# Silu experts with 352 rows per expert and an output projection in three fp16 matmuls

## The reference, cut to what matters

```python
# L3_ffn: 8 experts, top 2 per token, C = 128, hidden size H = 341
flat = layer_norm(t).reshape(-1, C)
probs = softmax(flat @ router_w.T)
topk_probs, topk_idx = top_k(probs, 2)
gates = scatter(topk_probs / (sum(topk_probs) + 1e-9))      # (tokens, 8), zero where not chosen
h = silu(einsum('nc,ehc->neh', flat, w1)) * einsum('nc,ehc->neh', flat, w3)
y = einsum('neh,ech->nec', h, w2)
t = t + einsum('ne,nec->nc', gates, y)
```

## Time and profile before

| | us |
|---|---|
| median of 3 runs | 4210.65 (4209.47 to 4216.52) |
| the profiled execution | 4210.06, span of the core 4208.3 |
| PE busy | 3396.0 (81%) |
| DVE, ACT, POOL busy | 2493.0 (59%), 1934.1 (46%), 862.6 (20%) |
| stage silu_experts | from about 3378.5 to the end |
| its POOL multiply, x352 | 451.6, mean 1.285 |
| its DVE multiply, x352 | 243.5, mean 0.692 |
| its ACT silu, x352 | 210.2, mean 0.597 |

### The profile page before, as it was taken

The page is one execution under the profiler, slowest core; times in us unless marked ns, Lnnn a source line. Parts: engine busy times, 40 slices in busy tenths (PEclk is TensorE's granted clock), DMA queues, the critical chain, the costliest instruction groups (busy, mean ns, idle before and its releaser), DMA issues. The chain is left out here.

```text
span 4208.3 us, 66480 instructions
## 1 busy us (share of the span) xinstructions
PE 3396.0 (81%) x24463; PEld 1527.2 (36%) x24463; DVE 2493.0 (59%) x4082; ACT 1934.1 (46%) x2321; POOL 862.6 (20%) x866
## 2 busy tenths in 40 slices
PE   6988777557687777777777777779978659999999
PEld 4655455324211111111111111253366524444444
DVE  3227667465588888888888888344367523333333
ACT  1215666512156666666666666533333213223332
POOL 0001333300000000000000000004400225555555
PEclk9997878878789999999999999979998779999999
DMA  4444454300400000000000000014400122322221
GB/s 138 132 120 95 108 113 109 84 1 6 174 11 14 20 18 22 20 14 20 17 22 15 20 15 15 19 34 153 138 1 0 42 78 80 97 89 84 85 82 47
DMA packets 137544, 247.17 MB, mean 59 GB/s; under 512 B 34808, under 2 KB 47264, under 8 KB 136800
## 3 DMA queue, kind: packets, MB, share of 16 engines
q1 hardware_dynamic: 137312, 243.98, 20.5%
HBM read 171.55 MB, written 56.62 MB: 54 GB/s over the span
## 5 line engine op out<-in xcount | busy, mean ns | idle before, releaser
L1073 DVE TENSOR_REDUCE mxv<-mx_ps 128x1 f32<-128x512 f32 x2048 | 1279.6, 682 | 240.7 <-PE mx_ps L932 240.6
L1048 ACT ACTIVATE PT<-st_ps 128x1024 f32<-128x1024 f32 x1024 | 992.5, 1021 | 450.2 <-PE st_ps L945 444.4
L932 PE MATMUL mx_ps<-KS,QS 24*128 24x512 f16 x2048 | 538.0, 391 | 318.0 <-DVE mxv L1073 300.4
L1921 DVE TENSOR_TENSOR u<-h_ps,s 128x512 f32<-128x512 f32 x352 | 243.5, 692 | 541.2 <-ACT s L1899 492.8
L959 PE MATMUL o_ps<-PT,VA 128*32 128x512 f32 x4096 | 547.2, 606 | 1.1 <-ACT PT L1048 0.9
L1951 POOL TENSOR_TENSOR hg<-u,gb 128x512 f32<-128x512 f32 x352 | 451.6, 1285 | 392.6 <-DVE u L1921 300.2
L1899 ACT ACTIVATE s<-h_ps 128x512 f32<-128x512 f32 x352 | 210.2, 597 | 586.9 <-PE h_ps L1875 586.9
L667 DVE TENSOR_REDUCE mxv<-mx_ps 128x4 f32<-128x512 f32 x512 | 319.9, 683 | 150.3 <-PE mx_ps L542 139.2
L1883 PE MATMUL y_ps<-hg,m_w 128*128 128x512 f32 x704 | 360.7, 596 | 56.4 <-POOL hg L1951 56.4
L932 PEld LDWEIGHTS mx_ps<-KS,QS 24*128 24x128 f16 x2048 | 136.9, 91 | 568.3 <-DVE mxv L1073 530.7
L945 PE MATMUL st_ps<-QS,KS 26*128 26x512 f16 x2048 | 326.9, 382 | 1.0 <-ACT PT L1048 0.2
(11 more groups left out here) (228 smaller groups left out, 4172.9 us busy)
## 6 DMA issues: line engine op xcount, KB each, us to landing
gb<-g SPq DMA_DIRECT2D x64, 512.0 KB, 3.7
gb<-g SPq DMA_DIRECT2D x16, 2048.0 KB
QK<-qk SPq DMA_DIRECT2D x128, 192.0 KB
qk<-hl SPq DMA_DIRECT2D x80, 256.0 KB, 3.3
RB<-d SPq DMA_DIRECT2D x48, 256.0 KB, 3.4
qk<-hl SPq DMA_DIRECT2D x64, 128.0 KB, 3.3
v<-vs SPq DMA_DIRECT2D x32, 256.0 KB
VS<-v SPq DMA_DIRECT2D x32, 256.0 KB, 3.1
```

Source lines behind the costliest of these rows:

```text
L932: nc.tensor.matmul(mx_ps[:, use % 3, :], rows(QS, g // 2, j, STACK)[:, t * C:(t + 1) * C], rows(KS, g // 2, j, STACK)[:, half * HALF:(half ...
L1048: nc.scalar.activation(PT[:, n % 2, 2 * a:2 * a + 2], st_ps[:, a], ACT.Exp, scale=1.0 / SHIFT ** 2).then_inc(st_free[a], 1)
L1073: nc.vector.tensor_reduce(mxv[:, g % 2, j, t, half:half + 1], mx_ps[:, slot], AX.X, ALU.max).then_inc(mx_free, 1)
```

## The change

Each expert is padded from 341 to 352 rows; 8 x 352 = 2816 rows are again 22 chunks. Six chunks are mixed instead of 7 (the cut at 1408 falls between chunks), with cuts at 96, 64, 32, 96, 64 and 32 rows, so 12 partial loads per half image instead of 14.

w2 is split too, times 256 into two fp16 parts. y(n) becomes three fp16 matmuls: w2 high and w2 low with the rounded hidden values `hh`, and w2 high with their rest `hl`. ACT makes hh(n) from hg(n) after silu(n+2), DVE makes hl(n) = hg(n) - hh(n) after u(n+2), and y follows h with a lag of four steps. hg has two slots instead of four, so hg(n) now waits for hl(n-2), where it waited for y(n-4). The order runs on across images: the last four y of an image stand between the first h of the next, and the second half is added at step 5 of the next image instead of after the last step. The first half is added at step 27 of its image, where it was at step 25.

w1 and w3 are loaded during the norm of O, rounded by ACT at its end (`early`), and subtracted and scaled by POOL during the last norm (`late`). w2 is loaded during the last norm; in `route` ACT first multiplies and rounds it, then stages XN, and POOL makes its rest. The gelu mixture's route, too, now rounds its weights before it stages XN.

```diff
-HID = 341
-CHUNKS = -(-E * HID // C)
+HID, HID_ROWS = 341, 352
+CHUNKS = E * HID_ROWS // C
 LO = 2.0 ** 11
+W2_UNIT = 2.0 ** 8
...
+            if late is not None:
+                @block.gpsimd
+                def _(pool):
+                    late.subtract(pool)
+
...
+                if early is not None:
+                    early.round(act)
...
+                if late is not None:
+                    late.set_lift()
...
+        self.nc, self.dram, self.split, self.plain = chip.nc, dram, split, plain
+        self.unit, self.lift_by = unit, lift
...
+    def round(self, act):
+
+        act.wait_ge(self.loaded, 16 * (len(self.split) + len(self.plain)))
+        for n, (_, hi, _) in enumerate(self.split):
+            if self.unit != 1.0:
+                self.nc.scalar.mul(self.full[:, n], self.full[:, n], self.unit).then_inc(self.scaled, 1)
+                act.wait_ge(self.scaled, n + 1)
+            self.nc.scalar.copy(hi, self.full[:, n]).then_inc(self.rounded, 1)
+
+    def set_lift(self):
+
+        self.nc.vector.memset(self.lift[:], self.lift_by).then_inc(self.set, 1)
+
+    def subtract(self, pool):
+
+        pool.wait_ge(self.set, 1)
+        for n, (_, hi, lo) in enumerate(self.split):
+            pool.wait_ge(self.rounded, n + 1)
+            self.nc.gpsimd.tensor_tensor(self.full[:, n], self.full[:, n], hi, ALU.subtract).then_inc(self.rest, 1)
+            pool.wait_ge(self.rest, n + 1)
+            copy_scaled(self.nc, lo, self.full[:, n], self.lift).then_inc(self.done, 1)
+        pool.wait_ge(self.done, len(self.split))
...
             def _(pool):
-                pool.wait_ge(lifted, 1)
...
-                sp.wait_ge(weights.loaded, weights.count)
...
             @block.scalar
             def _(act):
+                weights.round(act)
                 with act.Fori(0, B // 2) as i:
                     for s in range(2):
                         act.wait_ge(logits, i * 2 + s + 1)
                         nc.scalar.copy(xs[:, s], XN[:, i * 2 + s, :]).then_inc(staged, 1)
-                act.wait_ge(weights.loaded, weights.count)
-                for n, (_, hi, _) in enumerate(weights.split):
-                    nc.scalar.copy(hi, weights.full[:, n]).then_inc(w_hi, 1)
                 act.wait_ge(chain, 2)
...
-    first, last = c * C // HID, min((c + 1) * C, E * HID) - 1
-    return first, last // HID, (first + 1) * HID - c * C
...
-    H_SLOTS, HG_SLOTS, LAG = 2, 4, 2
+    H_SLOTS, P_SLOTS, CAST, LOW, LAG = 2, 4, 2, 2, 4
...
+        hg = chip.buf(ctx, "hg", [C, H_SLOTS, HALF])
+        hh, hl = (chip.buf(ctx, n, [C, P_SLOTS, HALF], F16) for n in ("hh", "hl"))
...
+                def output(i, n):
+                    s, c = n // CHUNKS, n % CHUNKS
+                    if c == 0:
+                        pe.wait_ge(added, i * 2 + s + 1)
+                    pe.wait_ge(rest, i * PER + n + H_SLOTS + 1)
+                    nc.tensor.matmul(y_ps[:, s], w2h[:, c, :], hh[:, n % P_SLOTS], start=(c == 0), stop=False)
+                    nc.tensor.matmul(y_ps[:, s], w2l[:, c, :], hh[:, n % P_SLOTS], start=False, stop=False)
+                    nc.tensor.matmul(y_ps[:, s], w2h[:, c, :], hl[:, n % P_SLOTS], start=False,
+                                     stop=(c == CHUNKS - 1)).then_inc(y_steps, 1)
+
+                def image(i, first):
+                    for n in range(PER):
+                        hidden_rows(i, n)
                         if n >= LAG:
-                            m = n - LAG
-                            s, c = m // CHUNKS, m % CHUNKS
-                            if c == 0:
-                                pe.wait_ge(added, i * 2 + s + 1)
-                            pe.wait_ge(gated, i * PER + m + H_SLOTS + 1)
-                            nc.tensor.matmul(y_ps[:, s], w2[:, c, :], hg[:, m % HG_SLOTS], start=(c == 0),
-                                             stop=(c == CHUNKS - 1)).then_inc(y_steps, 1)
-
-                with pe.Fori(0, B) as i:
-                    image(i)
+                            output(i, n - LAG)
+                        elif not first:
+                            output(i - 1, PER + n - LAG)
+
+                image(0, True)
+                with pe.Fori(1, B) as i:
+                    image(i, False)
+                for n in range(PER - LAG, PER):
+                    output(B - 1, n)
...
-                def image(i, last):
+                def round_hidden(i, n):
+                    act.wait_ge(gated, i * PER + n + H_SLOTS + 1)
+                    act.wait_ge(y_steps, i * PER + n + 1)
+                    nc.scalar.copy(hh[:, n % P_SLOTS], hg[:, n % H_SLOTS]).then_inc(cast, 1)
+
+                def image(i, first, last):
                     for n in range(PER):
                         act.wait_ge(h_ready, i * PER + n + 1)
                         nc.scalar.activation(s1[:, n % H_SLOTS], h_ps[:, n % H_SLOTS, 0], ACT.Silu).then_inc(silu_done, 1)
+                        if n >= CAST:
+                            round_hidden(i, n - CAST)
+                        elif not first:
+                            round_hidden(i - 1, PER + n - CAST)
                         if n == CHUNKS // 2:
...
+                image(0, True, False)
+                with act.Fori(1, B - 1) as i:
+                    image(i, False, False)
+                image(B - 1, False, True)
+                for n in range(PER - CAST, PER):
+                    round_hidden(B - 1, n)
...
-                def image(i, last):
+                def rest_of_hidden(i, n):
+                    v.wait_ge(cast, i * PER + n + 1)
+                    v.wait_ge(y_steps, i * PER + n + 1)
+                    nc.vector.tensor_tensor(hl[:, n % P_SLOTS], hg[:, n % H_SLOTS], hh[:, n % P_SLOTS],
+                                            ALU.subtract).then_inc(rest, 1)
+
+                def add(i, s):
+                    v.wait_ge(y_steps, i * PER + (s * CHUNKS + CHUNKS + P_SLOTS))
+                    at = X[:, i, s * HALF:(s + 1) * HALF]
+                    nc.vector.scalar_tensor_tensor(at, y_ps[:, s], 1 / W2_UNIT, at, ALU.mult, ALU.add).then_inc(added, 1)
+
+                def image(i, first, last):
                     for n in range(PER):
                         v.wait_ge(silu_done, i * PER + n + 1)
                         v.wait_ge(gated, i * PER + n + 1)
                         nc.vector.tensor_tensor(u[:, n % H_SLOTS], h_ps[:, n % H_SLOTS, 1], s1[:, n % H_SLOTS],
                                                 ALU.mult).then_inc(hidden, 1)
+                        if n >= LOW:
+                            rest_of_hidden(i, n - LOW)
+                        elif not first:
+                            rest_of_hidden(i - 1, PER + n - LOW)
                         if n == CHUNKS // 2:
                             low(i, 1)
                         if n == CHUNKS // 2 + CHUNKS and not last:
                             low(i + 1, 0)
+                        if n == LAG + 1 and not first:
+                            add(i - 1, 1)
...
-                            v.wait_ge(y_steps, i * PER + (CHUNKS + HG_SLOTS))
-                            at = X[:, i, 0:HALF]
-                            nc.vector.tensor_tensor(at, y_ps[:, 0], at, ALU.add).then_inc(added, 1)
-                    v.wait_ge(y_steps, i * PER + (PER + HG_SLOTS))
-                    at = X[:, i, HALF:N]
-                    nc.vector.tensor_tensor(at, y_ps[:, 1], at, ALU.add).then_inc(added, 1)
...
+                grant(nc, scratch, [(hidden, H_SLOTS), (gated, H_SLOTS), (rest, H_SLOTS), (y_steps, P_SLOTS), (added, 2)])
                 low(0, 0)
-                with v.Fori(0, B - 1) as i:
-                    image(i, False)
...
+                with v.Fori(1, B - 1) as i:
+                    image(i, False, False)
+                image(B - 1, False, True)
+                for n in range(PER - LOW, PER):
+                    rest_of_hidden(B - 1, n)
+                add(B - 1, 1)
...
-                        pool.wait_ge(y_steps, i * PER + n + 1)
-                        nc.gpsimd.tensor_tensor(hg[:, n % HG_SLOTS], u[:, n % H_SLOTS], gb[:, s, tile],
+                        pool.wait_ge(rest, i * PER + n + 1)
+                        nc.gpsimd.tensor_tensor(hg[:, n % H_SLOTS], u[:, n % H_SLOTS], gb[:, s, tile],
                                                 ALU.mult).then_inc(gated, 1)
...
+            wh, wl = (chip.buf(c2, n, [C, 2, CHUNKS, C], F16) for n in ("m3_wh", "m3_wl"))
+            w2h, w2l = (chip.buf(c2, n, [C, CHUNKS, C], F16) for n in ("m3_w2h", "m3_w2l"))
...
+                inner = Weights(chip, c3, dram, [(f"m3_w{2 * n + 1}", flat(wh[:, n]), flat(wl[:, n])) for n in range(2)], lift=LO)
+                with ExitStack() as c4:
+                    O = chip.buf(c4, "O", [C, B, N])
+                    local_attention(chip, XN, dram, identf, O)
+                    layer_norm(chip, O, mean_w, eps5, identf, X=X, gamma=gamma, beta=beta, fetch=inner, early=inner)
```

(64 more changed lines are left out.)

50 lines of the change are left out of this document (13 added, 37 removed).

## The result

| | before | changed |
|---|---|---|
| median | 4212.34 (4209.47 to 4216.52, 4 runs) | 4087.78 (4085.09 to 4091.84, 4 runs) |
| the profiled execution | 4210.06, span 4208.3 | 4087.38, span 4085.6 |
| stage: first gate issue | 3378.72 | 3369.37 |
| first hg | 3424.10 | 3386.26 |
| first hg to the end of the span | 784.2 | 699.3 |

A forecast was written before the change was run, and what follows sets the result against it. PE's matmul stream was taken as the bound: 3396.4 + 676.7 + 6.3 = 4079.4, with 3.97 after it 4083.4, less 6.6 a span of 4076.8, median 4079 us. Own range 4068 to 4090; with rivals 4066 to 4116.

The forecast's parts named there:

- The stream: Last stage, PE: a step falls from ten slots to nine, 1.937 us; 3144 slots, 676.7 us, remain.
- the sum: Forecast total: 4083.4 less 6.6 gives a span of 4076.8 us, 131.5 less than 4208.3.
- the loop heads: PE's loop jump at image ends: up to 0.32 us may show, six times, 1.9 us.
- The turn of hl and hg: Last stage, DVE and POOL alternate: 1.90 us a step, 0.04 under PE; nothing counted, +8 kept in the range.
- Rival 1: Loop heads and after xl: PE waits 2 to 4 us an image, +16 to +30, about 4100; chance 0.12.
- Rival 2: Last stage: hl and hg become the bound, a turn of 2.12 us, +64, 4143; chance 0.12.
- The gate load: Start of last stage: 3.67 MB over all sixteen engines lands 15.5 us after issue, at 3394.2.
- Ahead of the stage: Route, gelu route and norm of O before the last stage: together -6.6 us.
- Route's chain: Route, DVE: four operations beside POOL's splitting return to 0.69 us each, 12.7 us off the path.
- The norms: Norm of O covers ACT's 5.0 us but for 0.3; POOL's splitting beside the last norm costs nothing, 22 at most.
- rival 4: Ahead of the stage: the edit gives nothing back, POOL slows the last norm, +8 to +22, about 4093; chance 0.03.
- Rival 3: Last stage: partial loads stay on few engines, 45.4 us each, half images 54.3; 4274, 64 slower; chance 0.03.

The follow-up runs named there:

- e1: Changed kernel with four slots for hg instead of two; ratio to the kernel before 0.9678, first hg to end 689.6 us.
- e2: Changed kernel with hl computed from a zero tile in PSUM minus hh, its low part left out of the result; ratio 0.9654, first hg to end 689.9 us.
- e7: Changed kernel with w1 and w3 loaded during the last norm and split beside route again; ratio to the kernel before 0.9747.
- e4: Changed kernel with experts laid end to end at 341 rows again, 7 mixed chunks; ratio to the kernel before 1.0138, span 4276.4 us.

## Why the prediction was right, and where it was off

The mechanism of the gain and its size were right: 122.7 us less in the profiled span (4208.3 to 4085.6) where 131.5 were counted. By its steps:

- **The stream.** Right, with a little luck. The clock is 1.00, and e1 and e2, in which PE has the stage to itself, take 689.6 and 689.9 for the 689.2 of the sum. Two small errors cancel in that. PE's step is 1.9425 and not 1.937 (in e1 from 3401.24 to 4071.40 in 345 steps), since an fp16 matmul takes 0.2158 and the slot of 0.2153 was an average over a step with an fp32 matmul of 0.858: 1.9 us more. And the 1.9 us counted for the loop heads did not appear: in the changed kernel the first h of every image starts 1.94 after the one before it.
- **The turn of hl and hg.** This is the term that was mis-sized. Counted: 0.55 + 0.08 + 1.27 = 1.90, 0.04 under PE. Measured: 0.55 + 0.14 + 1.27 = 1.96, and 1.970 on average with the 15 turns of 2.28 beside an xl, 0.028 over PE's 1.9425. The 0.55 and the 1.27 were right; the 0.08 was the link from u to POOL, taken for hl to POOL. Over 351 turns that is 9.7 of the 10.2 us. With the counted link the xl would have found room: 21 turns of 1.90 and one of 2.22 average 1.915 (an estimate from these rows). The prediction kept +8 in its range for this place, so the bound was nearly right, and what was wrong was to take nothing as the likeliest with a reserve of 0.04, smaller than the uncertainty of a link. The ring binds at every step, so PE's slack of 1 us is used up early and helps no more.
- **Rival 1.** It priced stalls at loop heads and behind the xl at 2 to 4 us an image. The loop heads gave none. The stalls that PE has lie behind the add to X and behind the xl, from the seventh h on 9.1 us in 345 steps (679.3 for 670.2 in e1) or 1.2 an image, and e1 and e2 show that the ring makes them.
- **Rival 2.** Its idea, that hl and hg become the bound, came true; its price did not: full durations and a link on both sides would be 2.12, and the turn is 1.970. The Trainium skill, SBUF — State Buffer, section on who interferes with whom, names the right pair of instructions: a DVE instruction with two SBUF inputs contends with a GpSimd instruction that reads SBUF, and one with at most one SBUF input, outside DVE's two-port modes, does not. The runs agree: in e2 hl keeps 0.68 and hg 1.27 where they overlap. That the other is blocked for the whole instruction the page states of the two-port modes only, and of hl and hg it would be more than these runs show: hl ends 0.55 after hg, not 0.69, and in e1 POOL grows by 0.38 beside a DVE operation of 0.68.
- **The gate load.** 16.9 instead of 15.5. That the loads would go to all sixteen engines is right (share 1.01 at 263 GB/s). The second half's load is issued at 3378.20, 8.8 after the first, and must share the queues: from 3372 to 3386 alone 3.68 MB moved at the rate shown, as much as the whole first load, which had begun 2.6 before; what moved beside it can only be the second. I had counted the first load as if alone. That this is the 1.4 us is argued, not tested.
- **Ahead of the stage.** 9.35 instead of 6.6. Route's chain gives what was counted, all of it at 0.69, and e7 isolates 12.75 for 12.7. The two roundings for w2 cost less: 5.0 were counted, and the chain starts 3.4 later (3344.09 for 3340.66). The cover that I missed is in the row of PE's logits before:

```profile
3312.79 27.45 PE L1597 MATMUL l_ps<-wr,xs 128*128 128x8 f32 x128 [4.45 <-DMA wr<-in_m_router]
```

  PE was waiting for the router's weights from memory, so the first 1.6 us of ACT's delay hid behind a DMA. The rest of the 2.75, 1.1, was not isolated. The sum had 0.8 for the gelu route and 0.3 for the norm of O, and that norm ends at 3262.91 for 3263.2; but ahead of the stage executions differ by more than that.
- **The norms.** Covered as said. ACT rounds from 3257.31 on while DVE works to 3262.91, so even the 0.3 hid. Beside POOL's splitting, DVE's 16 subtractions and 16 multiplications of the last norm keep their mean of 0.688, and from the issue ahead of it to the load of the router's weights pass 46.42 us for 46.09, so rival 4 did not happen.
- **Rival 3.** Priced to within 3 us of e4's span, and rightly not the case here, as the load is on all engines with 352 rows.

The parts, each undone alone in the changed kernel, are worth 156 us of the stretch from the first hg to the end (the row counts, 854.9 less 699.3, and 29 more at the start), 36 (running on), 64 (three fp16 matmuls for one fp32), 12.75 (the split ahead). They don't add up to 123, since the faster stream is only worth something with the fast load: 17 steps of 1.94 are 33 us, less than the 46 of the slow load. Alone in the kernel before, the row counts gave 36.6 in the stage.

## What to carry to other kernels

Where two engines pass a tile back and forth over a ring as deep as their lag and also lock each other out of SBUF, add up the turn with a link for each pair of engines, and take a link that the trace doesn't show as uncertain by its own size (here it was 0.08 or 0.14 for one and the same pair, by whether the instruction itself carried the wait); if the reserve is smaller, expect the ring to bind, and give it two slots more or one operand in PSUM. Before a stream is made faster, see that each load behind it is shorter than the steps that hide it, for e4's loss came from exactly that. Cut partial loads at rows that spread over all DMA engines: here it took a load from 46 to 17 us for a few rows of padding.

## What was not expected of the hardware

- POOL starts 0.14 to 0.16 us after the end of the DVE operation it waits for where that wait stands in its queue ahead of the multiply, and 0.08 after it where the multiply carries the wait, for hl and for u alike.
- The one that comes second is held up for less than the other's remaining time would say: hl, with 0.68 of its own, ends 0.55 after hg; POOL, behind a DVE operation with about 0.5 left, takes 1.65, not the 1.8 of waiting first and then working 1.27.
- Which of the two is held up changes with who starts first: DVE in the changed kernel (mean 1.38 for hl), POOL in e1 (1.65 for hg, 0.68 for hl). With the same work DVE's mean hl fell by 0.65 us between them (1.38 to 0.73), so a third of DVE's 100% busy share was lock.
